# Draining the output banks on ScalarE and adding x on GpSimd instead of evicting them on VectorE

## What is computed

```
base  = y @ W.T + bias
h     = silu(y @ rw1.T + rb1);  logits = h @ rw2.T + rb2 + gates
coeff = softmax over the top 2 of 16 logits, 0 elsewhere
delta = sum over experts e of coeff[e] * (y @ A[e].T) @ B[e].T
out   = x + base + delta
```

## Time and profile before

| | |
|---|---|
| median of 3 runs | 741.69 us (741.21 to 742.25) |
| profiled execution | 742.07 us, its span 740.3 us |
| TensorE busy | 601.4 us, 81% of the span, 2624 matmuls |
| weight loads | 488.8 us, 66% |
| VectorE busy | 529.8 us, 72% |
| ScalarE busy | 352.3 us, 48% |
| GpSimd busy | 351.7 us, 48% |
| mean granted TensorE clock | 0.933 of full speed |
| DMA, mean | 101 GB/s |

### The profile page before, as it was taken

How to read it: one execution, slowest core, us unless ns; L and a number is a source line. 1 busy time by engine, 2 the same in 40 slices (tenths; PEclk the granted TensorE clock), 3 DMA queues, 4 the chain that set the end, 5 groups by cost and what they waited for, 6 DMA issues and landing times.

```text
span 740.3 us, 6922 instructions
## 1 busy us (share of the span) xinstructions
PE 601.4 (81%) x2624; PEld 488.8 (66%) x2624; DVE 529.8 (72%) x545; ACT 352.3 (48%) x403; POOL 351.7 (48%) x163
## 2 busy tenths in 40 slices
PE   0022225249899999999999999999999999999998
PEld 0011113138688868886888688868886888888886
DVE  5858799979977997799789978897889712120212
ACT  3756577674558355835574557455745430002000
POOL 0757787874475457544744475457444611000100
PEclk9975555659999999999999999999999999999999
DMA  5132334241353225323441344134413230222021
GB/s 202 55 113 74 120 108 142 85 129 56 102 164 119 72 100 160 125 70 101 140 145 62 110 143 142 52 119 138 146 40 132 80 105 1 85 76 67 0 86 71
DMA packets 30865, 74.74 MB, mean 101 GB/s; under 512 B 4336, under 2 KB 4464, under 8 KB 30832
## 3 DMA queue, kind: packets, MB, share of 16 engines
q1 hardware_dynamic: 30832, 74.31, 30.5%
HBM read 57.52 MB, written 16.78 MB: 100 GB/s over the span
## 4 chain that ended last, share of the span: by engine, by line
PE 57%; DVE 16%; POOL 15%; issue 7%; ACT 2%; DMA 1%; SPq 0%; DVEq 0%; POOLq 0%; ACTq 0%
PE acc L699 18%; PE acc L701 17%; PE acc L700 17%; POOL mix L458 4%; DVE mix L529 4%; DVE yr L555 3%; POOL kv L448 3%; POOL yr L453 3%; DVE mix L534 2%; POOL wx_lo L468 2%; DVE xo L562 2%; PE acc L711 2%; PE acc L710 2%; DMA kv<-f_cm 1%; POOL y_lo L462 1%
## 5 line engine op out<-in xcount | busy, mean ns | idle before, releaser
L699 PE MATMUL acc<-y_hi,wa_hi 128*128 128x512 f32 x640 | 258.6, 404 | 11.1 <-DVE xo L562 11.1
L700 PE MATMUL acc<-y_lo,wa_hi 128*128 128x512 f32 x640 | 254.8, 398 | 0.0
L701 PE MATMUL acc<-y_hi,wa_lo 128*128 128x512 f32 x640 | 254.2, 397 | 0.0
L699 PEld LDWEIGHTS acc<-y_hi,wa_hi 128*128 128x128 f32 x640 | 123.8, 193 | 44.3 <-DVE xo L562 18.8
L701 PEld LDWEIGHTS acc<-y_hi,wa_lo 128*128 128x128 f32 x640 | 123.5, 193 | 26.7
L700 PEld LDWEIGHTS acc<-y_lo,wa_hi 128*128 128x128 f32 x640 | 123.7, 193 | 25.3
L710 PE MATMUL acc<-y_hi,wr 128*128 128x512 f32 x64 | 28.1, 440 | 119.4 <-POOL y_lo L462 119.4
L458 POOL TENSOR_TENSOR mix<-mix,kv 128x1024 f32<-128x1024 f32 x31 | 74.0, 2388 | 96.4 <-DVE mix L513 73.8
L562 DVE SCALAR_TENSOR_TENSOR xo<-acc,bias_sb,xo 128x512 f32<-128x512 f32 x64 | 46.6, 736 | 76.4 <-PE acc L701 76.4
L462 POOL TENSOR_TENSOR y_lo<-yr,y_hi 128x1024 fp32r<-128x1024 f32 x32 | 76.5, 2392 | 49.1 <-ACT y_hi L308 49.1
L710 PEld LDWEIGHTS acc<-y_hi,wr 128*128 128x128 f32 x64 | 12.8, 200 | 125.7 <-POOL y_lo L462 123.5
(11 more groups left out here) (85 smaller groups left out, 770.9 us busy)
## 6 DMA issues: line engine op xcount, KB each, us to landing
kv<-f_cm SPq DMA_DIRECT2D x32, 512.0 KB, 3.6
yr<-x_cm SPq DMA_DIRECT2D x32, 512.0 KB, 3.3
xo<-x_cm SPq DMA_DIRECT2D x64, 256.0 KB, 3.9
out<-xo SPq DMA_DIRECT2D x64, 256.0 KB, 3.5
xo<-w_base SPq DMA_DIRECT2D x4, 512.0 KB, 4.0
xa<-w_base SPq DMA_DIRECT2D x4, 512.0 KB, 3.7
mix<-cond SPq DMA_DIRECT2D x1, 512.0 KB, 3.6
xo<-w_expert SPq DMA_DIRECT2D x1, 512.0 KB, 4.6
```

The lines of the kernel that those rows point to most:

```text
L699: nc.tensor.matmul(out_ap, wh, yh, start=start, stop=False)
L700: nc.tensor.matmul(out_ap, wh, yl, start=False, stop=False)
L701: return nc.tensor.matmul(out_ap, wl, yh, start=False, stop=stop)
```

## The change

Each block now takes two instructions. `drain` on ScalarE copies the bank with the bias into the second half of a buffer pair; `add_x` on GpSimd adds it to x in the first half, from which it is stored. `xo` becomes three pairs (the same memory), AHEAD becomes 2. TensorE's reuse of a bank waits for `drained` in place of `evacuated`. `evacuate` on VectorE goes.

```
-    XBUF = 6
-    AHEAD = 4
+    XBUF = 3
+    AHEAD = 2
...
-        xo = sb("xo", [P, XBUF, N])
+        xo = sb("xo", [P, XBUF, 2, N])
...
-        stage = [flat(xa), xo[:, 0:2, :].rearrange("p h c -> p (h c)")]
+        stage = [flat(xa), xo[:, 0, :, :].rearrange("p h c -> p (h c)")]
...
-                sp.dma_start(xo[:, e % XBUF, :], at(x_cm, e)).then_inc(x_in[e % XBUF], 16)
+                sp.dma_start(xo[:, e % XBUF, 0, :], at(x_cm, e)).then_inc(x_in[e % XBUF], 16)
...
-                sp.dma_start(at(out, e), xo[:, e % XBUF, :]).then_inc(out_stored[e % XBUF], 16)
+                sp.dma_start(at(out, e), xo[:, e % XBUF, 0, :]).then_inc(out_stored[e % XBUF], 16)
...
+            def drain(G, j):
+                e, bank = G * CB + j, out_bank(G, j)
+                act.wait_ge(out_done, e + 1)
+                if e >= XBUF:
+                    act.wait_ge(evacuated, e - XBUF + 1)
+                nc.scalar.activation(xo[:, e % XBUF, 1, :], acc[:, bank, :], ACT.Identity,
+                                     bias=bias_sb[:, j:j + 1]).then_inc(drained, 1)
...
+                ending = q == 0 and G > 0
+                if ending:
+                    drain(G - 1, 3)
+                    drain(G - 1, 4)
+                if q == 2 and routed:
+                    drain(G, 0)
+                    drain(G, 1)
                 if q == 1 and routed:
                     sigmoid_z(G)
...
                     scale_ends(s)
+                if ending:
+                    drain(G - 1, 5)
+                if q == 2 and routed:
+                    drain(G, 2)
                 if 0 < s <= UNITS and not late_split:
                     split_hi(s - 1)
...
                 if s + 1 < UNITS:
                     exp_k(s + 1)
+                if ending:
+                    drain(G - 1, 6)
+                    drain(G - 1, 7)
...
+            def add_x(G, j):
+                e = G * CB + j
+                pool.wait_ge(drained, e + 1)
+                pool.wait_ge(x_in[e % XBUF], 16 * (e // XBUF + 1))
+                nc.gpsimd.tensor_tensor(xo[:, e % XBUF, 0, :], xo[:, e % XBUF, 1, :], xo[:, e % XBUF, 0, :],
+                                        ALU.add).then_inc(evacuated, 1)
...
                     sum_n(s - 1)
                     gate_n(s - 1)
+                if ending:
+                    for j in range(3, 6):
+                        add_x(G - 1, j)
+                if q == 2 and routed:
+                    for j in range(3):
+                        add_x(G, j)
...
                     p1(s + 1)
+                if ending:
+                    for j in range(6, CB):
+                        add_x(G - 1, j)
...
-            def evacuate(G, j):
...
-                    pe.wait_ge(evacuated, (G - 1) * CB + 4)
+                    pe.wait_ge(drained, (G - 1) * CB + 4)
...
-                    pe.wait_ge(evacuated, G * CB + j - 4)
+                    pe.wait_ge(drained, G * CB + j - 4)
```

More of the change, by code:

```diff
@@ L198, in decay_mix_with_routed_lora_channel_major @@
         out_done = sem("out_done")
+        drained = sem("drained")
         evacuated = sem("evacuated")
@@ L642, in _ @@
                 routed = 0 <= G < GROUPS
[L643 to L646, removed]
                 if q == 1 and routed:
@@ L653, in _ @@
                     forward(s)
-                if ending:
-                    evacuate(G - 1, 5)
                 if q == 1 and routed:
@@ L659, in _ @@
                     routing(G)
-                if q == 2 and routed:
-                    evacuate(G, 0)
                 if s < UNITS:
                     forward_num(s)
[L664 to L667, removed]
                 if 0 < s <= UNITS:
                     ratio(s - 1)
[L670 to L673, removed]
                 if s == 0:
@@ L769, in _ @@
                     for a in range(2):
-                        pe.wait_ge(evacuated, (G - 1) * CB + 5 + a)
+                        pe.wait_ge(drained, (G - 1) * CB + 5 + a)
                         for kc in range(first):
@@ L778, in _ @@
                             low_rank(G, a, kc)
-                    pe.wait_ge(evacuated, (G - 1) * CB + 7)
+                    pe.wait_ge(drained, (G - 1) * CB + 7)
                     for kc in range(CB):
@@ L783, in _ @@
                 if G:
-                    pe.wait_ge(evacuated, G * CB)
+                    pe.wait_ge(drained, G * CB)
                 for kc in range(CB):
```

## The result

The changed kernel takes **795.88 us** (median of 4 runs, 795.67 to 796.32), the kernel before 741.66 (4 runs, 741.21 to 742.25): ratio 1.0731, 95% interval 1.0713 to 1.075. It is 54 us slower. The forecast was 810 with a range of 784 to 836, so the sign and the cause can be tested against a time that is 14 us better than forecast.

What follows compares the result with a forecast made beforehand. TensorE was taken to bound the kernel from the second group on; later loads and stores were to add 7.1, 49.0, 3.9 and 7.6, together 67.6 us, to the profiled 742.07: 809.7, say 810, range 784 to 836.

Steps and rivals of the forecast that it cites:

- SyncE, the part that decides: SyncE's queue: stores go out one landing apart, and the kv and r loads queued behind them wait too.
- first transition: First group's logits to the next group's, 77.46 us before: to become 84.6, with no late r load before it, +7.1.
- four groups: The four further groups in which a q = 0 step loads a unit: 86.8 us each instead of 74.55, +49.0.
- next transition: Into the next group, nothing loaded: late drain of block 3, 1.7, and the routing's 2.2 us wait, +3.9.
- end: Last stores, loads of x and adds after block 3's eviction: span to end at 747.9 instead of 740.3, +7.6.
- (a): Step 18: kv load behind block 0's store goes out 1.9 us later; the chain behind it moves by some 1.7.
- (b): Step 20: kv load waits behind stores 3 to 5, out at 381.7; ScalarE's exponential starts at 386.7, 9.6 later.
- (c): From the exponential to the routing: 10.7 us to VectorE's L572 instead of 9.5; L583 at 400.35, +10.0.
- (d): The r load behind stores 6 and 7 lands about 400.3; the routing waits another 2.2 us for its small exponential.
- Covered: Rival, chance 0.05: kv load of step 20 still out by about 372, TensorE stays the bound, 733.9 us.
- The floor: Rival, chance 0.12: same SyncE chain with landings of 2.0, 2.0 and 3.1 us, r load perhaps in time; 778 us.
- The clock's case: Rival, chance 0.10: idle time before the logits also lowers TensorE's clock, 4.6 us more in five groups; 833 us.

## Why the prediction was right, and where its sizes were off

*The mechanism.* "SyncE, the part that decides" held: the signs listed at its end are in the trace. The x load's wait for landings grew from 18.8 to 123.6 us, with two of them ahead of the kv load in the q = 0 step shown; that load went out 8.0 us behind the gate (some 9 forecast); the exponential waits 9.02 us; TensorE waits before base 0 and before the logits and no longer at blocks 5 and 6. One sign held in part: at block 7 TensorE still waited in three groups, 3.2 us in all, for the drain of block 2, the one that the prediction held to come late. That the order, not the work, is at fault was argued then and is shown now, by the kernel with both loads first.

*The sum, term by term.* The span grew by 53.6 us (740.3 to 793.9), forecast 67.6:

| term | forecast | measured |
|---|---|---|
| first transition | +7.1 | +7.2 (84.67 - 77.46) |
| four groups | +49.0 | +38.4 (336.57 - 4 x 74.55) |
| next transition | +3.9 | +1.5 (76.05 - 74.55) |
| end | +7.6 | +6.3 |

The four groups hold three quarters of the miss of 14 us. That the first row fits to 0.1 us is luck: in that stretch, too, the exponential came 12.4 us behind the gate (223.78 to 236.18) and not 13.8, so something else there took longer than forecast; what it was stays open. The shortest of the four groups, 83.61 against 86.8, by steps:

- (a) The kv load of step 18 went out at 358.80, 1.67 us behind its gate, as worked out (1.9). But it was used 3.56 us later, where the row of before had 4.50 (337.63 to 342.13). So the chain moved by 0.7 and not by 1.7: 1.0 too much.
- (b) Gate to exponential took 12.5 us, not 13.8: the first store landed in 2.04 (2.4 taken; the two rows named for it are 2.51 apart), the second in 3.41 (3.3), kv in 4.56 (5.0), the add and the store came 0.2 sooner, and SyncE needed 0.4 less between the transfers: 1.3 too much.
- (c) From that exponential to the routing were 13.46 us, 13.65 forecast.
- (d) The routing's wait for its exponential, at the head of this stretch behind the logits at 331.71, was 1.34 us, 2.2 forecast: 0.9 too much.

*The prices.* GpSimd's add took 1.29 us (1.30 taken). ScalarE's drain took 0.682 us, between the two bounds, 0.59 and 0.75, and nearer to the one I did not take. The two drains on the path, 6 and 7, took 1.25 us for the 1.2 of the sum, so that moved next to nothing. No table load came with it: their counts are the same in both kernels.

*The landings by the rows or by the page.* The three on the path measured 2.04, 3.41 and 4.56, together 10.0; the rows gave 10.7. The fit of the Trainium skill (DMA: Bandwidth & Descriptors, Anatomy of one DMA) gave 8.4, and 798 us in all, both estimates. The trace does not agree with it, 2.04 where it has 2.6, 3.41 for 2.6 and 4.56 for 3.2, so its nearer total is luck: it comes from errors elsewhere that happened to be of the other sign.

*The rivals.* "Covered" would have been right about the mechanism with the loads in front: that kernel takes 738.8, not 733.9, because its groups take 73.4 us on average (238.22 to 531.74 in four) and not 71.9. The floor's landings of 7.1 us did not occur in the group shown. The clock's case came half true: the clock fell, but in the group looked at that cost nothing. After 3.97 us of idle time the logits of group 1, at 247.57, took 1.88 us, where the kernel before took 1.06, and the stretches behind them, in the columns of the earlier trace rows, show the granted clock:

```profile
249.00:253.00 4.00, 4.00 (x12) 3.19 (x12) 2.26 (x16) 3.42 (x6) 1.55 (x1) 0.50 0.36 109
254.00:257.00 3.00, 3.00 (x14) 2.44 (x14) 2.97 (x4) 0.00 (x0) 0.00 (x0) 1.00 0.00 0
```

0.50 is the lower of 1.2 and 2.4 GHz, 1.00 the higher; between them TensorE worked without a pause. The Trainium skill (TensorE: Matmul & The Clock Gate, Part 1) holds that the array is slow by default and that activity frees it, and this trace agrees. But the clock was back before the spread at 257.05, VectorE scanned and formed a unit's y meanwhile and did not wait for that spread. Not even the 0.82 us of the longer logits came onto the path: they ended at 249.45, and VectorE was in its forward scan until 249.71. The last group of the five began with logits at full speed (1.06 us, after 1.28 of idle time) and still took 84.07.

## What to carry to other kernels

When an output path gets longer, look at what stands behind its stores in the same in-order queue: a load that the next unit needs pays for every wait ahead of it, here 57 us for two loads (795.9 - 738.8). Put such loads ahead of the stores first, and only then judge the buffers and the engine that evicts. A queue's total waiting time did not tell the cost here; compare the time at which a load could go out (here the gate's end) with the time at which it did.

## What the runs showed of the hardware that I had not expected

- The same transfer took longer the more was in flight beside it, by an amount that decides here: a kv load of 512 KB was used 4.56 us after its issue behind the three stores, 6.06 with an r load of the same size issued 0.47 behind it, and 3.56 when only one store of 256 KB went out just ahead.
- SyncE's queue waited 121, 124 and 145 us for landings in kernels that took 745.9, 795.9 and 738.8 us.
- A drain with the bias on ScalarE, 0.682 us, costs nearly as much as VectorE's eviction with bias and x in one instruction, 0.75 us; the 64 evictions of one engine become 42.3 us on ScalarE and 81.3 on GpSimd.
